# A quantised self-attention on one core: the exponentials' scale from a ScalarE register, and finished pairs of heads copied from PSUM by ScalarE

## What is computed

```python
def fq_floor(x):                                  # one step for the whole tensor
    s = exp2(ceil(log2(max(abs(x)) / 127)))
    return clip(floor(x / s), -128.0, 127) * s
dots = fq_floor(einsum('bhnd,bhmd->bhnm', q, k) * temp)
attn = fq_floor(softmax(dots, axis=-1))
out  = einsum('bhnm,bhmd->bhnd', attn, v)
out  = fq_floor(fq_floor(out) @ fq_round(w_out))
```

## Time and profile before

| what | us |
|---|---|
| median of 3 runs | 3149.09 |
| lowest and highest | 3144.04, 3150.22 |
| the profiled execution, device time | 3145.82 |
| its span in the trace | 3144.0 |
| share of the span busy: TensorE, VectorE, ScalarE, GpSimd | 85%, 80%, 46%, 5% |

### The profile page before, as it was taken

One profiled execution on the slowest core, in us unless ns is written; L12 is line 12 of the kernel. 1 busy time (PEld: TensorE's weight loads), 2 busy tenths in 40 slices (PEclk: granted clock), 3 DMA queues, 4 the chain that ended last, 5 costly groups with the idle time before them and its releaser, 6 DMA issues. The chain is left out here.

```text
span 3144.0 us, 44439 instructions
## 1 busy us (share of the span) xinstructions
PE 2659.6 (85%) x13112; PEld 1034.6 (33%) x13160; DVE 2504.7 (80%) x4278; ACT 1443.7 (46%) x2366; POOL 159.0 (5%) x147
## 2 busy tenths in 40 slices
PE   7999999967777747777769699999999379999997
PEld 4444432211111124444335222222224234444443
DVE  5988679999998979999888688888868854444454
ACT  3320043318999989999423255555530011211111
POOL 0000043310000000000000000111100000000000
PEclk9999999975555569999989899999999679999999
DMA  8561122214333333333125433434356200000000
GB/s 314 167 224 64 40 97 94 93 80 141 127 120 122 111 103 116 104 116 104 57 71 184 114 106 99 115 98 116 114 182 248 69 27 27 28 27 27 27 27 27
DMA packets 196495, 324.41 MB, mean 103 GB/s; under 512 B 32281, under 2 KB 118297, under 8 KB 187025
## 3 DMA queue, kind: packets, MB, share of 16 engines
q1 hardware_dynamic: 192160, 306.12, 30.0%
q10 hardware_dynamic: 4208, 16.78, 1.4%
HBM read 192.32 MB, written 130.51 MB: 103 GB/s over the span
## 5 line engine op out<-in xcount | busy, mean ns | idle before, releaser
L1398 DVE TENSOR_REDUCE stats<-bank 128x1024 f32 (+1 forms) x352 | 408.0, 1217 | 60.5 <-PE bank L845 28.1
L1260 ACT ACTIVATE arena<-arena,scale 128x512 bf16<-128x512 int8 x512 | 408.1, 799 | 53.4 <-DVE arena L1638 53.4
L905 PE MATMUL bank<-arena 64*128 64x512 bf16 x512 | 306.4, 605 | 104.9 <-DVE arena L1631 66.9
L1278 ACT ACTIVATE arena<-arena,scale 128x512 f32<-128x512 int8 x512 | 370.5, 803 | 13.1 <-DMA arena<-dq_scr 11.0
L1631 DVE CUSTOM_DVE_ANT_0 arena<-bank,arena,fac 128x512 int8<-128x512 f32 x512 | 349.8, 747 | 23.2 <-PE bank L905 10.2
L1785 DVE TENSOR_REDUCE arena<-bank 128x2 f32<-128x1024 f32 x256 | 312.5, 1223 | 54.7 <-PE bank L997 38.8
L1342 ACT ACTIVATE arena<-bank 128x1024 f32<-128x1024 f32 x256 | 248.0, 1022 | 189.4 <-PE bank L1013 189.4
L1376 ACT ACTIVATE arena<-bank,arena,fac 128x512 f32<-128x512 f32 x128 | 99.5, 777 | 458.8 <-PE bank L1165 458.8
L1041 PE MATMUL bank<-arena 128*32 128x512 f32 x2048 | 270.9, 606 | 0.0
L1248 ACT ACTIVATE arena<-bank,floor_c,fac 128x1024 int8<-128x1024 f32 x96 | 115.6, 1205 | 337.8 <-PE bank L845 287.2
L1986 DVE TENSOR_SCALAR arena<-arena 128x512 f16<-128x512 f32 x128 | 54.7, 428 | 260.7 <-ACT arena L1376 260.7
(11 more groups left out here) (202 smaller groups left out, 3477.5 us busy)
## 6 DMA issues: line engine op xcount, KB each, us to landing
dq_scr<-arena SPq DMA_DIRECT2D x128, 256.0 KB, 2.0
arena<-dq_scr SPq DMA_DIRECT2D x128, 256.0 KB, 2.7
arena<-half_scr SPq DMA_DIRECT2D x256, 128.0 KB, 2.8
qkv_scr<-arena SPq DMA_DIRECT2D x8, 3072.0 KB, 9.7
arena<-in_x SPq DMA_DIRECT2D x16, 1024.0 KB, 8.4
half_scr<-arena SPq DMA_DIRECT2D x32, 512.0 KB, 4.1
arena<-qkv_scr SPq DMA_DIRECT2D x128, 128.0 KB, 2.2
x_scr<-arena SPq DMA_DIRECT2D x16, 1024.0 KB, 4.5
```

The lines of the kernel that those rows point to most:

```text
L905: return mm(dst, qE[r, h // 2, P * t:P * t + P], kE[r, h // 2, :], start=True, stop=True)
L1260: last = A(e_dump[:, NT * (h % 2) + t, :], dq8[:, h % 4, t, :], ACT.Exp, bias=negm_b[:, par, c:c + 1], scale=scale[:, S_DOTS:S_DOTS + 1], ...
L1278: A(eG[:, s % 2, t, :], dqG[:, s % 4, t, :], ACT.Exp, bias=negm_g[:, par, c:c + 1], scale=scale[:, S_DOTS:S_DOTS + 1]).then_inc(S("eG_done ...
L1398: return V.tensor_reduce(dst, src, ax, ALU.max, apply_absolute_value=True)
```

## The change

It has two parts. The scale of the exponentials in stages 6 and 7 is no longer a column of 128 numbers in SBUF: ScalarE loads the one number (the step of the scores is the same for all rows) once into a register, behind the barrier that ends stage 5, and both exponentials name the register. The bias remains a column. And the copy of a finished pair in stage 7 goes from VectorE to ScalarE: `pair_out` becomes an ACTIVATE of the kind Copy, with the same wait on `pvG_mm` and the same increment. On ScalarE it stands behind the four exponentials of each odd step s (from s = 3 of the first batch on), for the pair of heads s-3 and s-2; the last pair of all comes behind the loop. VectorE keeps F, T and the peaks.

```diff
--- before.py
+++ after.py
@@ -1251,6 +1251,9 @@
             barrier(act, 5)
 
 
+            exp_scale = nc.scalar.alloc_register("exp_scale")
+            nc.scalar.load(exp_scale, scale[0:1, S_DOTS:S_DOTS + 1].bitcast(I32))
+
             def sums(b, par):
                 for h in range(H):
                     act.wait_ge(S("sum_done"), b * H + 4 + h - 1)
@@ -1258,7 +1261,7 @@
                     for t in range(NT):
                         c = NT * h + t
                         last = A(e_dump[:, NT * (h % 2) + t, :], dq8[:, h % 4, t, :], ACT.Exp, bias=negm_b[:, par, c:c + 1],
-                                 scale=scale[:, S_DOTS:S_DOTS + 1], accum_out=sum_b[:, par, c:c + 1])
+                                 scale=exp_scale, accum_out=sum_b[:, par, c:c + 1])
                     last.then_inc(S("sum_done"), 1)
             batches(act, sums)
             act.wait_ge(S("rows_kept"), NB)
@@ -1266,6 +1269,10 @@
             act.wait_ge(S("log_done"), 1)
             A(sum_back, log_sum, ACT.Exp, scale=-1.0).then_inc(S("log_done"), 1)
             barrier(act, 6)
+
+            def pair_out(b, p):
+                act.wait_ge(S("pvG_mm"), b * H + 16 + 2 * p + 2)
+                A(pair_of_o(b * PAIRS + p), bank[:, 4 + p % 4, :], ACT.Copy).then_inc(S("oG_evac"), 1)
 
             def weigh(b, par):
                 for s in range(H):
@@ -1276,8 +1283,11 @@
                     for t in range(NT):
                         c = NT * s + t
                         A(eG[:, s % 2, t, :], dqG[:, s % 4, t, :], ACT.Exp, bias=negm_g[:, par, c:c + 1],
-                          scale=scale[:, S_DOTS:S_DOTS + 1]).then_inc(S("eG_done"), 1)
+                          scale=exp_scale).then_inc(S("eG_done"), 1)
+                    if s % 2 and not (is_batch(b, 0) and s < 3):
+                        pair_out(b, (s - 3) // 2)
             through(act, weigh)
+            pair_out(NB, -1)
             barrier(act, 7)
 
             for b in range(NB):
@@ -1666,10 +1676,6 @@
                                 PT[h % 2].rearrange("p a b -> p (a b)"), -129.0, None, ALU.add
                                 ).then_inc(S("aTG_done"), 1)
 
-            def pair_out(b, p):
-                dve.wait_ge(S("pvG_mm"), b * H + 16 + 2 * p + 2)
-                V.tensor_copy(pair_of_o(b * PAIRS + p), bank[:, 4 + p % 4, :]).then_inc(S("oG_evac"), 1)
-
             def pair_peak(b, p):
                 dve.wait_ge(S("oG_evac"), b * PAIRS + 4 + p + 1)
                 amax(stats[:, bass.ds(b * PAIRS + p, 1)], pair_of_o(b * PAIRS + p)).then_inc(S("oG_peak"), 1)
@@ -1687,15 +1693,12 @@
                         row_factors(b + 1, 1 - par)
                     if not (is_batch(b, 0) and s < 1):
                         turned_out(b, s - 1)
-                    if s % 2 and not (is_batch(b, 0) and s < 3):
-                        pair_out(b, (s - 3) // 2)
                     if s % 2 == 0 and not (is_batch(b, 0) and s < 4):
                         pair_peak(b, (s - 4) // 2)
             row_factors(0, 0)
             through(dve, floor_weights)
             turned_out(NB, -1)
             pair_peak(NB, -2)
-            pair_out(NB, -1)
             pair_peak(NB, -1)
             dve.wait_ge(S("oG_peak"), NB * PAIRS)
             link(amax(peak[:, S_O:S_O + 1], stats[:, 0:NB * PAIRS]))
```

## The result

| | before | changed |
|---|---|---|
| median, us | 3146.95 (4 runs) | 3201.84 (4 runs) |
| lowest to highest | 3144.04 to 3150.22 | 3198.85 to 3202.84 |
| span of the profiled execution | 3144.0 | 3201.1 |
| stage 6, first tile to the last copy of row maxima | 416.8 | 410.8 |
| stage 7, first exponential to the start of the last V | 379.5 | 444.9 |

The changed kernel is slower: the ratio is 1.0173, with a 95% interval of 1.0155 to 1.019, or 54.9 us between the medians. Stage 6 gives 6.0 us back and stage 7 takes 65.4 more; together 59.4, where the spans differ by 57.1. The rest lies in stages that the change does not touch; these differ by up to a few microseconds from kernel to kernel, with either sign.

A forecast was written before the change was run, and what follows sets the result against it. Stage 6 was taken as bound by ScalarE, stage 7 by VectorE with ScalarE almost level. +66 - 13 = +53 on 3145.8 gave 3198.8; with 3.3 for the median, 3202, own range 3188 to 3216, wider range 3183 to 3245.

The forecast's parts named there:

- The price of a column: ScalarE's exponentials in stages 6 and 7: a register instead of the scale column saves 90 ns each, 0.80 to 0.71 us.
- Stage 6, -13: Stage 6: VectorE becomes the bound at 6.06 us a pair; sums end at 1115.2 instead of 1128.75, gain 13 us.
- the two stalls where the loop turns round: VectorE in stage 6: stalls of 3.86 and 3.79 us, hidden before by ScalarE's heads in hand, now count, 7.7 us.
- Stage 7, the new wait, +66: Stage 7: ScalarE's copy waits for V(s-2), holding up E(s+1); two heads take 6.91 us instead of 5.86, +66 us.
- The ring: Stage 7: copy in step s, E(s+1), F(s+1), T(s), V(s), copy in step s+2; 6.91 us for two heads.
- One page speaks against the move: Stage 7's copy: the skill's rule would make it up to 2.0 us on ScalarE, 87 us more; the rows contradict it.
- The register brings nothing: Rival, chance 0.12: stage 6 stays as it is, stage 7 has 0.36 us more per two heads; +88, 3237 us.
- TensorE's clock falls: Rival, chance 0.09: longer pauses in stage 7 lower TensorE's clock, W and V slow, up to 92 us more, 3294.
- V is in time: Rival, chance 0.04: stage 7's copy waits for nothing, ScalarE's 5.43 us for two heads sets the pace; 3109 us.

The follow-up runs named there:

- the register alone: Against the kernel before: both exponentials take the scale from a register, the pair's copy stays on VectorE; 3138.01 us, ratio 0.9976.
- Stage 6 written out: Against the changed kernel: VectorE's part of stage 6 written out for all eight batches, no hardware loop; 3185.23 us, ratio 1.0131 to the kernel before.
- the additional copy: Against the changed kernel: one more 128x512 copy, read by nobody, on ScalarE behind each pair's copy (3276.09 us) or ahead of its wait (3201.23 us).
- the copy a step later: Against the changed kernel: ScalarE's pair copy moved behind the exponentials of even s, for heads s-4 and s-3; 3104.47 us, ratio 0.9871 to the kernel before.
- the copy alone: Against the changed kernel: scale of both exponentials a column again, pair's copy still on ScalarE; 3259.02 us, ratio 1.0358 to the kernel before.
- the filled pause: Against the kernel with column scale and ScalarE's pair copy: 16 transposes of a constant on TensorE at each odd step's end; 3242.17 us, ratio 1.0307.

## Why the prediction was right

The changed kernel was forecast at 3202, measured at 3201.84. The nearness is partly luck, since errors cancelled. Stage 6 gained 7 us less than forecast. Against that, the median of before, on which the forecast stood, came out 2 us lower with a fourth run, and the stages that are not touched gave 4.5 us back between the medians (2.3 between the profiled executions), for which the forecast had nothing.

*The price of a column.* Taken as 90 ns, measured 91 and 93. Right, and the register alone shows nothing on the other side.

*Stage 6, -13.* Measured -6.0. ScalarE did cease to be the bound, VectorE did become it, and the two stalls where the loop turns round did count (3.88 and 3.78). The step that failed is VectorE's 6.06 us a pair: I read it from the part that is written out and put VectorE's small waits in the loop down to ScalarE. They are VectorE's own: in the loop most pairs take 0.07 to 0.17 us more, and nine of 48 some 0.5 more. Stage 6 written out is 15.7 us shorter, 7.7 for the two stalls and 8.0 for these pauses. The reading that later VectorE waits for ScalarE to free a slot was wrong too: in the kernel before, its pairs in the loop already took 6.13 to 6.30 us for the most part, and of its waits only 0.3 us in all were put down to ScalarE. From its first tile to its last, VectorE took 406.3 us before the change (711.9 to 1118.2) and takes 403.6 in the changed kernel (711.4 to 1115.0). It nearly set the pace already, and the rest of the 6 us is ScalarE's shorter run behind it (9.29 us, now 5.88).

*Stage 7, the new wait, +66.* Measured +65.4. The ring was forecast at 6.91 us; from the copy at 1147.90 to that at 1577.82, 62 turns took 429.9, or 6.93 each. Its terms, from the turn shown, with the forecast in brackets: copy to E 0.49 (0.51), E to F 2.68 (2.70), F to T 1.20 (1.19), T to V 1.37 (1.45), V 1.02 (1.02), V's end to the copy 0.04 (0.04). They make 6.80; a turn in the loop takes 6.88. ScalarE's wait was forecast at 1.3 to 1.5 us, 63 times, and 90 in all; 59 of the 63 are 1.31 to 1.50, the other four 1.81 to 2.62, and together they make 90.8. That the wait and not the work costs the time is shown by the additional copy on either side of it, and by the copy a step later.

*One page speaks against the move.* The Trainium skill (ScalarE: Activation LUTs, Rules for kernel authors) puts plain arithmetic such as `add` and `mul` on VectorE, with a factor of up to about 3 for bf16. Here the pair's copy, float32 from PSUM, took 0.60 us on ScalarE and 0.68 on VectorE, and moved a step later it brought 33.5 us over the register alone. For this copy, with VectorE full and the register in place, the rows decide against the rule.

*The register brings nothing.* Fallen. The kernel that this rival describes is the copy alone: it took 3259, where the rival gave 3237. Stage 7 grew by 123.6 us in place of the rival's 88; the 36 us above it are the turns that the clock made longer, which the rival left out. The register's worth depends on the place: 7 us when alone in a kernel bound by VectorE; 57 us between the copy alone and the changed kernel; 51 us with the copy a step later (3155.86 to 3104.47), where ScalarE sets the pace in stage 7 with eight exponentials a turn, 62 x 0.74 = 46, and 6 come from stage 6.

*TensorE's clock falls.* Not the main mechanism, yet it was nearer than its chance of 0.09 said. Four of the 62 turns in the changed kernel take 7.29 to 8.19 us, 3.4 us in all above 6.88. In the longest, V takes the lower level's 1.92 us, and W, at 1.51, lies partly in it:

```profile
1304.32 1.51 PE L922 MATMUL bank<-identb,arena 128*128 128x128 bf16 x16 [1.81 <-DVE arena L1690]
...
1305.76 1.92 PE L933 MATMUL bank<-arena 128*64 128x512 bf16 x4
...
1307.84 0.60 ACT L1275 ACTIVATE arena<-bank 128x512 f32 x1 [2.60 <-PE bank L933]
```

In the copy alone, where a turn would take 7.25 us, 37 of 62 were longer. My argument against it, that TensorE at the lower level is full and gets the clock back, was right as far as it goes: the clock comes back each time, and the price is paid again in a later turn. The Trainium skill (TensorE: Matmul & The Clock Gate, A second HAM failure mode) describes such an oscillation from short idles between groups of matmuls; the copy alone shows it, at a clock of 0.86, and the filled pause takes it away.

*V is in time.* Fallen as it stood; moved by one step, the copy is in time, and its 5.38 us for two heads is what this rival gave (5.43).

## What to carry to other kernels

Before a piece of work is moved to an engine with room, write down what its wait stands behind on the old engine and what will stand behind it on the new one, and follow the chain from there back to the same wait: if it closes, the sum around it is the pace, however idle the engines are. The cure here was not to move the work back but to place it one step later, where the chain has had time. An engine's pace in a hardware loop is read inside of the loop, since its pauses may hide behind another engine's pace until that one is made quicker.

## What I had not expected of the hardware

The clock's sensitivity: with turns of 6.88 us and a long pause of TensorE of 1.63 us in most of them the granted clock stays at 0.98, with turns of 7.25 and a pause of 2.00 it is 0.86. The pause alone does not tell when it falls: in the changed kernel three of the four falls came behind a pause of 1.8 us and one behind 1.63, and at least two other pauses of 1.8 had no fall behind them. So 0.36 us more of ScalarE in the ring cost 58 us of stage 7, of which the ring itself explains 22 or 23. And 1024 transposes of a constant, work for nothing, made the kernel 17 us quicker.

The overlap of ScalarE's instructions: in the copy a step later the exponentials are 758 ns long by the median, up to 902, where they were 710 in the changed kernel, and yet two heads with a copy take 5.38 us, with the starts of the exponentials 0.61 apart in both. So the pace is to be read from start to start. What fills the longer durations no run here tells.
